# Turning the gathered rows of slots 3 to 16 with DMA transposes in a routed feed-forward stage, in place of transposes on the matmul engine

## The reference, cut to what matters

```python
def reference(x, Wqkv, b_qkv, Wout, b_out, w_router, w_fc, w_proj):
    # x: (8, 512, 512) float32, 4096 tokens of width 512
    xn = layernorm(x)                                   # (x - mean) / sqrt(var + 1e-5)
    # attention, 16 heads of 32, with ALiBi bias, causal, biases on qkv and out
    s = softmax(q @ k.T * scale + bias, causal) @ v @ Wout.T + b_out
    # feed-forward with 2 experts of hidden size 2048, each token goes to one
    logits = xn @ w_router.T
    top_idx, top_weight = argmax(softmax(logits)), the probability at it
    h = xn @ w_fc[top_idx].T
    a = square(where(h >= 0, h, 0.5 * h))
    f = (a @ w_proj[top_idx].T) * top_weight
    return x + s * silu(f)
```

## Time and profile before

| what | value |
|---|---|
| median of 3 runs | 1481.97 us (1479.03 to 1482.86) |
| the profiled execution, its time | 1481.51 us |
| its span in the trace | 1479.7 us |
| granted TensorE clock over the span | 0.987 of full |
| PE busy | 1384.0 us, 94% |
| DVE, ACT, POOL busy | 923.9, 770.7, 682.5 us (62%, 52%, 46%) |
| costliest line | L1106, `up`, 368.0 us |
| second | L1126, `down`, 363.9 us |

### The profile page before, as it was taken

How to read it: one execution, slowest core, us unless ns; L and a number is a source line. 1 busy time by engine, 2 the same in 40 slices (tenths; PEclk the granted TensorE clock), 3 DMA queues, 4 the chain that set the end, 5 groups by cost and what they waited for, 6 DMA issues and landing times.

```text
span 1479.7 us, 30039 instructions
## 1 busy us (share of the span) xinstructions
PE 1384.0 (94%) x9863; PEld 880.8 (60%) x9863; DVE 923.9 (62%) x2441; ACT 770.7 (52%) x1824; POOL 682.5 (46%) x896
## 2 busy tenths in 40 slices
PE   2889999999999999999689999999999999999995
PEld 1455555655555565555456666666666666666663
DVE  7577777777777777777759745555444555544444
ACT  3478778787777878787736422222222222222221
POOL 0356667465666746566523433333333333323332
PEclk9989999999999999999999999999999999999998
DMA  4425334343534434245346311110011111010100
GB/s 161 144 86 148 125 115 125 110 139 100 171 101 130 128 106 138 89 141 140 107 164 207 115 44 44 44 43 25 23 41 42 39 44 44 30 29 30 36 30 30
DMA packets 84897, 133.45 MB, mean 90 GB/s; under 512 B 14095, under 2 KB 63247, under 8 KB 82576
## 3 DMA queue, kind: packets, MB, share of 16 engines
q1 hardware_dynamic: 75808, 105.70, 23.0%
q0 software_dynamic: 8944, 25.83, 5.6%
HBM read 97.81 MB, written 33.95 MB: 89 GB/s over the span
## 4 chain that ended last, share of the span: by engine, by line
PE 75%; DVE 10%; POOL 6%; ACT 3%; issue 3%; DMA 1%; DVEq 1%; SPq 0%; ACTq 0%; POOLq 0%
PE psY L1126 19%; PE psF L1106 19%; PE psA L352 19%; PE psT L446 7%; PE psA L461 5%; POOL pr L941 4%; PE psS L425 3%; DVE sg L1303 2%; PE psX L1080 1%; POOL route L969 1%; PE psA L409 1%; DVE stat L749 1%; DVE am L636 1%; ACT stage L519 1%; DVE wf L1225 1%
## 5 line engine op out<-in xcount | busy, mean ns | idle before, releaser
L1106 PE MATMUL psF<-xT,wf 128*128 128x256 f16 (+1 forms) x3264 | 368.0, 269 | 0.0
L1126 PE MATMUL psY<-wf,aT 128*128 x1584 | 363.9, 379 | 0.3 <-DVE aT L1270 0.3
L1106 PEld LDWEIGHTS psF<-xT,wf 128*128 x3264 | 312.0, 98 | 63.5
L1344 POOL TENSOR_TENSOR a<-a 128x512 f32<-128x512 f32 (+1 forms) x136 | 153.1, 1126 | 392.1 <-DVE a L1261 390.5
L941 POOL TENSOR_SCALAR pr<-pr,rden 128x128 f32<-128x128 f32 (+3 forms) x512 | 268.4, 542 | 141.9 <-DVE rden L868 140.3
L579 ACT ACTIVATE pr<-pr,mn 128x128 f32<-128x128 f32 (+3 forms) x512 | 281.9, 553 | 0.0
L857 DVE CUSTOM_DVE_ANT_0 pr<-psS,base,nsl 128x128 f32<-128x128 f32 (+3 forms) x512 | 249.6, 543 | 4.2 <-PE psS L425 4.2
L1126 PEld LDWEIGHTS psY<-wf,aT 128*128 128x128 f16 x1584 | 154.5, 98 | 158.5 <-issue 1.0
L446 PE MATMUL psT<-conf,pr 128*128 128x128 f32 x1280 | 205.7, 279 | 18.1 <-POOL pr L941 16.5
L1183 ACT ACTIVATE rl<-psF 128x512 f32<-128x512 f32 (+1 forms) x136 | 79.3, 583 | 263.2 <-PE psF L1106 263.0
L446 PEld LDWEIGHTS psT<-conf,pr 128*128 128x128 f32 x1280 | 157.3, 143 | 81.3 <-POOL pr L941 27.3
(11 more groups left out here) (155 smaller groups left out, 1371.0 us busy)
## 6 DMA issues: line engine op xcount, KB each, us to landing
qk_parts<-pre SPq DMA_DIRECT2D x64, 256.0 KB, 2.8
qs<-qk_parts SPq DMA_DIRECT2D x128, 128.0 KB, 2.7
ks<-qk_parts SPq DMA_DIRECT2D x128, 128.0 KB, 2.7
wst<-in_wf SPq DMA_DIRECT2D x16, 1024.0 KB
wstage<-in_wf SPq DMA_DIRECT2D x32, 512.0 KB, 4.6
xin<-in_x SPq DMA_DIRECT2D x32, 256.0 KB, 4.4
attn_out<-so SPq DMA_DIRECT2D x32, 256.0 KB, 2.0
pt<-in_wqkv SPq DMA_DIRECT2D x4, 768.0 KB, 10.1
```

What stands on the lines that cost most here:

```text
L1106: last = nc.tensor.matmul(psF[c % 2][:, k * TT:k * TT + tn], w(e, 2 * hc, hl, kc * 512 + col, P), xT[:, r % 2, x, kc, 0:tn], start=(m == 0 ...
L1126: last = nc.tensor.matmul(psY[r % 2][h][:], aT[:, c % 4, x, k, h * P:(h + 1) * P], w(e, 2 * hc + 1, hl, q * 512, 512), start=(c == 0 and k ...
L1344: nc.gpsimd.tensor_tensor(at, at, at, ALU.mult).then_inc(s["a_ready"], 1)
```

## The change

For slots 3 to 16 the float32 transposes on PE go. The half is normalized two slots ahead, in parts 4 (half 0) and 6 (half 1) of step m - 2 for slot m; ScalarE and VectorE split it unturned, in parts 5 and 7, into `xs`, which is the memory of staging buffer 0 of the weights seen as float16; and SP turns it with DMA transposes of 128x128 float16 blocks from `xs` into `xT`, 8 for each half (4 blocks of the width, high and low). Slots 0 to 2 are turned as before. `up` waits for the DMAs' semaphores `turned_in[h]` in place of `X_lo`.

```diff
@@ att_sync, after all else that SP does
         for i in range(QB):
             sp.wait_ge(s_out[i], 16 * (B + 1))
+        ffn["turn"](sp)
@@
+BY_DMA = 3
+def turned_at(n, c, what):
+    if n < 0:
+        return
+    at = {(0, 0): (1, 0), (2, 0): (1, 1), (2, 1): (1, 0), (4, 1): (1, 1),
+          (4, 0): (2, 0), (6, 0): (2, 1), (5, 1): (2, 0), (7, 1): (2, 1)}.get((c, what))
+    if at is None:
+        return
+    m = n + at[0]
+    if (m < BY_DMA if at[0] == 1 else m >= BY_DMA) and m < SLOTS and at[1] < halves(m):
+        yield m, at[1]
@@ ffn_block
+    xs = wstage[:, 0, :].bitcast(F16).rearrange("p (h x d) -> p h x d", h=NH, x=2)
+    turned_in = [sem(f"turned_in{i}") for i in range(NH)]
+    def turn(sp):
+        for n in range(BY_DMA, SLOTS):
+            for h in range(halves(n)):
+                sp.wait_ge(s["X_lo"], n * NH + h + 1)
+                if h == 0:
+                    sp.wait_ge(s["F_done"], (n - 1) * GR)
+                for x in range(2):
+                    for kc in range(KC):
+                        sp.dma_start_transpose(xT[:, n % 2, x, kc, h * P:(h + 1) * P],
+                                               xs[:, h, x, kc * P:(kc + 1) * P]).then_inc(turned_in[h], 16)
+    def rows_turned(eng, n, h):
+        eng.wait_ge(turned_in[h], (n - BY_DMA + 1) * 2 * KC * 16)
@@ up, on PE
-            if c == 0:
+            if c == 0 and n < BY_DMA:
                 wait(pe, s["X_lo"], n * NH + halves(n))
+            if c == 0 and n >= BY_DMA:
+                for h in range(halves(n)):
+                    rows_turned(pe, n, h)
@@ step, on PE
-                if c in (1, 3) and n >= 0 and ahead and (c - 1) // 2 < halves(n + 1):
+                if c in (1, 3) and n >= 0 and ahead and n + 1 < BY_DMA:
                     xtrans(pe, n + 1, (c - 1) // 2)
@@ turn_hi, on ScalarE
+        if n >= BY_DMA:
+            act.wait_ge(s["ln_done"], n * NH + h + 1)
+            if n == BY_DMA:
+                act.wait_ge(s["ws_lo"], len(order))
+            else:
+                rows_turned(act, n - 1, h)
+            nc.scalar.activation(xs[:, h, 0, :], xn[:], ACT.Copy, scale=1024.0).then_inc(s["X_hi"], 1)
+            return
@@ step, on ScalarE (VectorE alike, with turn_lo, and with what = 0 for norm)
-                if c in (2, 4) and 0 <= n < SLOTS - 1 and (c - 2) // 2 < halves(n + 1):
-                    turn_hi(act, n + 1, (c - 2) // 2, r + 1)
+                for m, h in turned_at(n, c, 1):
+                    turn_hi(act, m, h, m % 4)
@@ norm, on VectorE
-        wait(dve, s["X_done"], n * NH + h)
+        k = n * NH + h
+        wait(dve, s["X_done"], min(k, BY_DMA * NH))
+        if k > BY_DMA * NH:
+            dve.wait_ge(s["X_hi"], k)
+            dve.wait_ge(s["X_lo"], k)
@@ turn_lo, on VectorE
+        if n >= BY_DMA:
+            stt(out=xs[:, h, 1, :], in0=xn[:], scalar=1024.0, in1=xs[:, h, 0, :],
+                op0=ALU.mult, op1=ALU.subtract).then_inc(s["X_lo"], 1)
+            return
```

More of the change, by code:

```diff
@@ L1290, in step @@
                            ALU.mult, ALU.mult).then_inc(s["z_ready"], 1)
-                if c in (2, 4) and 0 <= n < SLOTS - 1 and (c - 2) // 2 < halves(n + 1):
-                    turn_lo(dve, n + 1, (c - 2) // 2, r + 1)
+                for m, h in turned_at(n, c, 1):
+                    turn_lo(dve, m, h, m % 4)
                 nh, ch = ahead_of(n, c, 1)
@@ L1315, in step @@
                     fetch(dve, n + 2, r + 2)
-                if c in (0, 2) and 0 <= n < SLOTS - 1 and c // 2 < halves(n + 1):
-                    norm(dve, n + 1, c // 2, r + 1)
+                for m, h in turned_at(n, c, 0):
+                    norm(dve, m, h, m % 4)
             assert not done or k[0] == 2 + halves(n - 1), k[0]
@@ L1361, in ffn_gpsimd @@
         pool.wait_ge(s["out_done"], ((SLOTS - 1) * NH + 1) * 16)
-    return {"sync": load, "pieces": len(order), "xtrans": xtrans, "tensor": ffn_tensor, "split_hi": split_hi,
+    return {"sync": load, "turn": turn, "pieces": len(order), "xtrans": xtrans, "tensor": ffn_tensor, "split_hi": split_hi,
             "turn_hi": turn_hi, "scalar": ffn_scalar, "split_lo": split_lo, "fetch": fetch, "norm": norm,
```

## The result

The changed kernel took **1466.41 us** (median of 4 runs, 1463.73 to 1467.07) beside 1482.41 for the kernel before (the three runs behind the 1481.97 on record, and a fourth); the ratio is 0.9892 with a 95% interval of 0.9877 to 0.9906. Run again later, five rounds on one chip, it was 0.9897 (0.9883 to 0.9911). The forecast was 1466.5, in a range of 1463 to 1472.

What follows compares the result with a forecast made beforehand. The prediction took PE's matmul stream to bound the feed-forward stage; removing 27 halves of transposes saves 9.2 + 6.2 = 15.4 us, all else hidden, so 1481.97 - 15.4 = 1466.5 us, range 1463 to 1472.

Steps and rivals of the forecast that it cites:

- What bounds the kernel: Feed-forward stage from step 2 on: PE's stream alone, busy 599.21 of 600 us; what leaves it shortens the time.
- What leaves PE, 15.4 us: Slots 3 to 16: 27 transposed halves leave PE, 13 x 0.71 for half 0 plus 14 x 0.44, 15.4 us.
- T, the time of a DMA transpose: SP's queue: what one more transpose adds when they follow each other; taken as 0.6 us, 9.6 us per slot.
- The point of decision, T = 2.6: At chunk 0's `up`: DMA transposes stay hidden and cost nothing up to 2.6 us each, over four times the value taken.
- rival 1: DMA transposes become the bound at chunk 0's `up`, making the kernel slower, 1487 or about 1650 us; chance 9%.
- The helpers: ScalarE, VectorE and GpSimd beside PE: a chunk's low part some 0.1 us late against 6.39 us of slack, costing nothing.
- the start of slot 3: Step 1, where weight splits still run: the chunk's low part late by 0.3 us or a little more, costing nothing.
- The gather: Norm comes 4 parts after the gather instead of 8; 8 to 9 us of cover remain, costing nothing.
- Rivals 2 and 3: Late helper or gather gives back 3 to 10 us, chance 6%; lower PE clock gives back 12 us, chance 2%.

Runs made afterwards that it cites:

- experiment 2: Changed kernel with 108 float32 transposes of constants put back on PE at the old places, without waits: 1476.69 us, 0.9975 of the kernel before.
- experiments 2 and 3: The second of the two: kernel before with its PE transposes one part later, splits and half 1's norm moved, no DMA transposes: 1474.92 us, 0.9964.
- experiment 10: Changed kernel with one DMA per half, slot 2 also turned by DMA, slot 1's half 0 one part later on PE: 1460.53 us, 0.9864; again 1462.55, 0.9880.
- experiment 5: Changed kernel with all blocks turned twice, 32 DMA transposes per slot instead of 16: 1485.95 us, 1.0034 of the kernel before.
- experiment 6: Changed kernel with extra DMA transposes into free staging memory, 48 per slot instead of 16: 1752.16 us, 1.1825 of the kernel before.
- experiment 4: Changed kernel with each high block turned once more, 24 DMA transposes per slot instead of 16: 1464.24 us, 0.9877 of the kernel before.

## Why the prediction was right

- **What bounds the kernel.** Right: PE was busy 585.00 of 585 us after the change too, so what left it shortened the time. That the median lies within 0.1 us of the forecast is luck: run again, the same change took 15.7 us off (1481.05 to 1465.31), and kernels with the same PE stream had medians from 1464.24 to 1466.41.
- **What leaves PE, 15.4 us.** Right in sum, and in both terms: experiment 2 puts the transposes at 0.43 per half, where the distance of neighbours gave 0.44, and experiments 2 and 3 show that the other 0.27 of half 0 was the wait for the norm. The feed-forward stage went from 707.34 us (755.36 to 1462.70, first `up` to last `down`) to 691.55, 15.8 less: 15.4 as forecast, and 0.44 from slot 1's half 0, which the change does not touch (1.28 before, 0.84 after) and the forecast did not have. PE reached that stage 0.67 us later in this execution (756.03), and 15.1 is left in the span.
- **T, the time of a DMA transpose.** This term was mis-sized: 0.6 taken, 1.31 to 1.35 measured (means of a slot or of a whole kernel), held by SP's issue. The step that failed was to price it by packets of the DMA engines. Their time is in fact small: SP's queue took 25.6% of 16 engines' 1464.6 us in place of 23.0% of 1479.7, which is 554 us of engine time for 216 transposes, 0.16 us of all 16 engines each, for 0.57 by my working: the queue has 160 packets more per block, not 128, at 0.016 us each, not 0.07. The page "VectorE: DVE Perf Modes" of the Trainium skill (the three transpose paths) has 1309 ns; the traces agree (1.31 us in the slot shown), and it was nearer than my row. The number was right all the same because the sum hung only on the point of decision.
- **The point of decision, T = 2.6.** Shown from both sides: at 24 transposes (31 to 32 us per slot) nothing, at 32 (43.0) the time of before is passed by 0.3%, at 48 the queue is the bound. What was varied is the number of transposes, not T itself. The margin was twofold, not over fourfold as I wrote, so rival 1 was nearer than the working for its 9% said.
- **The helpers.** The chunk's low part is 0.23 us late for the 0.1 forecast, and by another way: not through ScalarE's wait for the norm, but through GpSimd's squaring, 1.27 for 1.04, which the prediction names as a possible cost of less than 1 us. At the start of slot 3 it was 1.2 for 0.3, through a split of weights that takes 2.06. Both stayed under their cover.
- **The gather.** Right: the longest landing of `xg` was 6.0 us, the second gather of the slot starts at 941.36 and the norm at 956.97, so 9.6 us of cover were left.
- **Rivals 2 and 3.** No late gather or helper at PE, and the clock stayed at 1.00 over the stretch. That SP has nothing else to issue in this stretch held, and experiment 10 shows that two DMA transposes can stand even among its weight loads, at 0.7 us of PE's time. Which of that step's changes took the 0.7 stays open.

## What to carry to other kernels

Price an instruction in a full stream by the distance of its neighbours, with and without it, and part that distance into work and wait: almost a quarter of this gain was a wait that a shift by one part removes without any DMA. For an operation that the trace doesn't show, work out at which price it would decide before settling on a value; here a value wrong by a factor of two did no harm, and one more factor of two would have. And put as many blocks as the layout lets you into one DMA transpose: it won no time here, where the queue was hidden, but it left the queue free for 39 of 42 us.

## What the runs showed of the hardware that was not expected

- A DMA transpose holds SP's queue for about 1.23 us whether it turns 1, 4 or 8 blocks of 128x128 float16; back to back, single ones come 1.31 to 1.35 us apart on the mean.
- The mean is not a steady pace. Most single transposes start 1.27 or 1.28 us apart, and one in 11 to 16 takes 1.5 to 2.7 us by itself: 18 of 216 in the changed kernel, 39 of 432 in experiment 5, 41 of 648 in experiment 6. So the mean over 8 in a row lies anywhere between 1.26 and 1.47. The runs don't show the load of the queue as the cause: the changed kernel and experiment 4, whose queues rest in every slot, have 1.34 over their halves, and experiment 6, whose queue never rests, 1.32. What holds the long ones stays open. A price read from one stretch (1.31) was 0.035 us too low per transpose, which was 15 us in experiment 5.
- In experiment 6 PE sat idle for 18.5 to 21.8 us before each first `up`, and that `up` took 4.08 to 5.30 us in place of 2.78. One of the two longest, at 1027.31 after 19.59 us, ran at or near the lower of the two clock levels (1.2 GHz) almost throughout; the next `up`, at 1035.09, took 2.78 again. By busy time and clock in stretches (the columns of the earlier trace rows) the granted clock is 0.66 over the idle stretch with its edges, 0.53 in the six microseconds in which this `up` runs, and 1.00 for the rest of the slot:

```profile
1005.00:1027.00 22.00, 2.72 (x14) 1.03 (x11) 1.38 (x2) 1.23 (x2) 1.04 (x1) 0.66 0.12 25
1027.00:1033.00 6.00, 5.69 (x27) 3.83 (x28) 0.00 (x0) 0.35 (x1) 0.00 (x0) 0.53 0.13 27
1033.00:1068.00 35.00, 35.00 (x243) 23.52 (x242) 19.71 (x30) 10.54 (x18) 14.65 (x13) 1.00 0.28 71
```
